# Per-example mixing matrices: one batch on TensorE at the front, or two VectorE operations inside each step

## The chip, the cores and the metric

The kernel runs on one core of a Trainium2 chip. The metric is device time in microseconds (us). Before the change it is 2982.37 us, the median of 3 runs (2981.94 to 2983.42). Engines are named as in the profile: PE is TensorE (PEld its weight loads), DVE is VectorE, ACT is ScalarE, POOL is GpSimd, SP is SyncE, which only issues DMAs (SPq).

## What is computed

There are 128 examples x[j] of 128 channels by 2048 time points, in float32. Each passes four residual layers. Layers 0 and 2 mix the channels with a matrix of the example's own: eight fixed 128x128 matrices, weighted by a softmax of a small MLP on the example's condition. Layers 1 and 3 are grouped convolutions of 9 taps over time.

```
h   = gelu(gelu(cond @ W0 + b0) @ W1 + b1)
att = softmax(h @ W2 + b2)                           # 8 weights an example
agg_w = einsum('bk,koi->boi', att, weight[..., 0])   # the example's matrix
agg_b = att @ bias_k
x = x + einsum('boi,bih->boh', agg_w, x) + agg_b     # layers 0 and 2
x = x + conv(x, weight, 9 taps, 4 groups) + cond @ c_weight.T + side   # layers 1 and 3
```

## The kernel before, in words

**Tiling.** Every tensor is split into a high part (rounded to the type that TensorE multiplies at speed) and a low part (the rest), and each product is three passes: high by high, high by low, low by high. Four 32-row tiles of the array work side by side (t = 0 to 3), each three rounds behind the one before. One layer's result for one example is four banks of 128x512: mixing layers use banks 0 to 3, convolutions banks 4 to 7. A step has 96 rounds of 4 matmuls: 12 for layer 0, 36 for layer 3, 12 for layer 2, 36 for layer 1. The identity of each residual is inside the weights.

**Steps.** Step i works on layers 0 and 1 of example i, layer 2 of example i-1 and layer 3 of example i-2. Steps -1 to 2 and 126 to 129 are unrolled, and a hardware loop runs the rest. Each engine has its own program in a fixed order, and semaphores tie them. In step i:

- DVE writes the low parts of layer 1 (`low(1, i-1)`) and of layer 0 (`low(0, i)`), four operations each (L587); then `x_high(i+1)`, four casts of the next example (L596), which wait for its load; then `low(2, i-1)`.
- ACT evacuates the high parts (L438), casts both mixing matrices (L444) and evacuates layer 3 into `o_ph` (L464), which raises `phases_set`.
- POOL writes the matrices' low parts (L628), `x_low(i+1)` (four operations, L635), and `in_time(i-2)` (L642), which puts the result into time order in `o_t`.
- SP issues, in this order: four loads of layer 2's matrix (L198), the 16 shuffles of example i-2 that bring `o_ph` to `o_ch` (L228, after `phases_set`), `load_x(i+2)` (four DMAs, L203, after `x_low(i+1)` has freed `x_t`), four loads of layer 0's matrix, the store of the output (L236).

**Mixing matrices.** All 256 of them are made before the first step. The attention is transposed and masked; TensorE multiplies 64 times (L279) with eight kernels' matrices laid over the partitions; ACT (L412) and DVE (L558) evacuate the results into stages of 2 MB; DVE adds the diagonal (L564); SP stores eight such stages into the scratch `mixed` in DRAM (L194). The steps then load 64 KB four times a matrix. The stages, the small inputs and the output buffers share the tile `work`.

Of the kernel before, what the change touches and what calls it, by code (L numbers as in the profile page):

```python
# [5 lines left out]
def build_cond_resid(nc, x, small, mix_w, mix_b, conv_w, consts, scratch, out):  # L6
# [7 lines left out]
    PH = 4  # L14
# [5 lines left out]
    SMALL = small.shape[1]  # L20
    NL = 4
    Q = 4
    QW = C * C // Q
    QB = QW // N
# [3 lines left out]
    LOADS = 3  # L28
    CHUNKS = 4

    ctx = ExitStack()
    with ctx:
# [12 lines left out]
        work = sb("work", [128, 5, QW])  # L45
        o_ph = work[:, 0, 0:T].rearrange("c (g n) -> c g n", g=G)
        o_ch = work[:, 0, T:2 * T].rearrange("c (p n) -> c p n", p=PH)
        o_t = work[:, 1, 0:T]
        m_raw = {l: sb(f"m_raw{l}", [128, G, C]) for l in (0, 2)}
        m_parts = {l: sb(f"m_parts{l}", [128, 2, G, C], f32r) for l in (0, 2)}  # L50
        bias = [sb(f"bias{l}", [128, G]) for l in range(NL)]
        conv_parts = {l: sb(f"conv_parts{l}", [128, 2, SHIFTS, 128], f32r) for l in (1, 3)}
        bias_table = sb("bias_table", [128, B, NL * G])
        ps = ctx.enter_context(nc.psum_tensor("ps", [128, 8, N], fp32))


        conv_raw = sb("conv_raw", [128, SHIFTS * 128])
        consts_sb = sb("consts_sb", [128, 166])
        ident = consts_sb[:, 0:128]
        w_low = consts_sb[:, 128:129]  # L60
        a_low = consts_sb[:, 129:130]
        in_quarter = consts_sb[:, 130:134]
        ident_g = consts_sb[:, 134:166]

# [4 lines left out]
        mix_raw = [work[:, 2, :], work[:, 4, :]]  # L69
        mix_high = flat(xp, "r g n")  # L70
        mix_parts = flat(y1, "r p n")[:, 0:QW]
        room_r = flat(y2, "r g n")
        room = work[:, 3, :]

        stage = [work[:, k, :] for k in range(5)]
        SLOT = (0, 1, 3, 2, 3, 4, 2, 4)
        taken = {"room": 0, "room_r": 0}
        def part_of(name, shape):

            width = 1  # L80
            for n in shape[1:]:
                width *= n
            first = taken[name]
            taken[name] += width
            view = (room if name == "room" else room_r)[0:shape[0], first:first + width]
# [5 lines left out]
        emb_sb = part_of("room", [128, B])  # L91
        mlp_w_sb = part_of("room", [128, 4, 128])
        ctx_w_sb = part_of("room", [128, 2, G, 128])
        mlp_b_sb = part_of("room", [128, 4])
        w2_sb = part_of("room", [128, 2, K])
        b2_sb = part_of("room", [128, 2, K])
        side_sb = part_of("room", [128, G])
        assert taken["room"] == SMALL
        mix_b_sb = part_of("room", [K, 2, 128])
        hidden0 = part_of("room", [128, 2, B])  # L100
        hidden1 = part_of("room", [128, 2, B])
        att_rep = part_of("room", [128, 2, 128])
        att_t = part_of("room", [128, 2, B])
        att_high = part_of("room_r", [128, 2, B])
        att_parts = part_of("room_r", [128, 2, B])
        att_q = part_of("room_r", [128, 2, Q, B])
# [5 lines left out]
        small_in = sem("small_in")  # L112
        mix_in = [sem(f"mix_in{l}") for l in range(2)]
        conv_in = sem("conv_in")

        hid0_mm, ctx_mm, hid1_mm = sem("hid0_mm"), sem("ctx_mm"), sem("hid1_mm")
        logit_mm, att_t_mm, mix_b_mm = sem("logit_mm"), sem("att_t_mm"), sem("mix_b_mm")
        agg_mm = sem("agg_mm")

        hid0_set, hid1_set, expo_set = sem("hid0_set"), sem("hid1_set"), sem("expo_set")  # L120
        mix_high_set, conv_high_set = sem("mix_high_set"), sem("conv_high_set")
        agg_act = sem("agg_act")
# [3 lines left out]
        att_t_set, att_q_set, mix_b_read = sem("att_t_set"), sem("att_q_set"), sem("mix_b_read")  # L126
        mix_set, conv_ident_set, conv_set = sem("mix_set"), sem("conv_ident_set"), sem("conv_set")
        agg_dve = sem("agg_dve")
        agg_set = sem("agg_set")
        zeros_set = sem("zeros_set")  # L130
        stored = [sem(f"stored{s}") for s in range(len(stage))]
# [13 lines left out]
        in_time_set = sem("in_time_set")  # L145

# [22 lines left out]
        def uses(n):  # L169

            return SLOT[:n].count(SLOT[n])

        def by_phase(q):

            return ps[:, q, :].rearrange("c (m p) -> c p m", p=PH)

# [7 lines left out]
        def _(sp):  # L184
            sp.dma_start(room[:, 0:SMALL], small).then_inc(small_in, 16)
            sp.dma_start(consts_sb[:], consts).then_inc(small_in, 16)
            sp.dma_start(mix_b_sb, mix_b).then_inc(small_in, 16)
            sp.dma_start(mix_raw[0], mix_w[0]).then_inc(mix_in[0], 16)
            sp.dma_start(conv_raw[:], conv_w[0]).then_inc(conv_in, 16)
            sp.dma_start(mix_raw[1], mix_w[1]).then_inc(mix_in[1], 16)  # L190

            def store_quarter(n):
                sp.wait_ge(agg_set, n + 1)
                sp.dma_start(scratch[n // Q][:, n % Q * QW:(n % Q + 1) * QW], stage[SLOT[n]]).then_inc(stored[SLOT[n]], 16)  # L194

            def load_matrix(layer, j):
                for q in range(G):
                    sp.dma_start(m_raw[layer][CG * q:CG * (q + 1)],  # L198
                                 scratch[layer // 2][bass.ds(j, 1)].rearrange("s (g c o) -> (s c) g o", g=G, c=CG)).then_inc(m_in[layer], 16)

# [4 lines left out]

            load_x(0)
            for n in range(Q):
                store_quarter(n)
            sp.wait_ge(conv_set, 1)
            sp.dma_start(conv_raw[:], conv_w[1]).then_inc(conv_in, 16)  # L210
            for n in range(Q):
                sp.wait_ge(stored[SLOT[n]], 16 * (uses(n) + 1))
            for n in range(Q, 2 * Q):
                store_quarter(n)
            for n in range(Q, 2 * Q):
                sp.wait_ge(stored[SLOT[n]], 16 * (uses(n) + 1))
            load_matrix(0, 0)
# [27 lines left out]
        def _(pe):  # L245
# [27 lines left out]
            for n in range(2 * Q):  # L273
                for m in range(QB):
                    if m % (QB // CHUNKS) == 0:
                        pe.wait_ge(mix_set, n // Q * CHUNKS + m // (QB // CHUNKS) + 1)
                    if n:
                        mixed_out(n - 1, m)
# [471 lines left out]
```

## Time and profile before

| | |
|---|---|
| median of 3 runs | 2982.37 us |
| the profiled execution, own time | 2982.91 us |
| its span | 2981.1 us |
| busy share of the span: PE, DVE, ACT, POOL | 97%, 44%, 52%, 52% |
| mean granted TensorE clock | 0.985 of full speed |
| DMA | 493.88 MB, 166 GB/s |

A busy share says how long an engine was at work, not whether something waited for it. The page's line of 40 slices has PE at 9 tenths from the second slice on; only the first slice (4) and the last (7) are lower. An operation's mean duration times its count is its busy time, and the idle time before a group, with its releaser, says what it waited for.

### The profile page before, as it was taken

To read this page: it belongs to the slowest core of one execution; us is meant where nothing else is said; L and a number is where in the kernel's file an instruction comes from. 1 tells how busy PE (TensorE), PEld (TensorE's weight loads), DVE (VectorE), ACT (ScalarE), POOL (GpSimd) and SP (SyncE) were. 2 spreads that over 40 slices of the span, in tenths; PEclk is the share of its full clock that TensorE was granted. 3 is DMA by queue.
4 is the path that set the end of the run, shared out by engine and by line. 5 is a ranking of instruction groups with operands and counts; after the bars stand their busy time and mean duration, and the time that the engine had idled before them with its cause. 6 is when DMAs were issued, how large, how long until landed. Compare 5 with 4: busy or idle time off the path is not lost.

```text
span 2981.1 us, 121239 instructions
## 1 busy us (share of the span) xinstructions
PE 2905.9 (97%) x49252; PEld 2885.6 (97%) x49252; DVE 1312.3 (44%) x2142; ACT 1552.4 (52%) x2358; POOL 1551.1 (52%) x1796
## 2 busy tenths in 40 slices
PE   4899999999999999999999999999999999999997
PEld 2799999999999999999999999999999999999996
DVE  5344444444444444444444444444444444444441
ACT  4455555555555555555555555555555555555552
POOL 0455555555555555555555555555555555555552
PEclk7899999999999999999999999999999999999998
DMA  7465665665665665665665655655655656656653
GB/s 312 106 178 157 163 173 157 165 171 158 165 170 158 166 169 158 167 168 158 171 164 158 173 162 158 175 160 158 178 157 159 179 156 161 178 155 162 176 156 110
DMA packets 339978, 493.88 MB, mean 166 GB/s; under 512 B 59624, under 2 KB 190832, under 8 KB 322288
## 3 DMA queue, kind: packets, MB, share of 16 engines
q1 hardware_dynamic: 339952, 493.51, 60.9%
q8 instruction: 19, 0.31, 0.0%
q14 instruction: 7, 0.06, 0.0%
HBM read 208.06 MB, written 150.99 MB: 120 GB/s over the span
## 4 chain that ended last, share of the span: by engine, by line
PE 97%; DMA 1%; DVE 1%; ACT 0%; SPq 0%; issue 0%; POOL 0%; POOLq 0%; DVEq 0%; ACTq 0%
PE ps L317 72%; PE ps L302 24%; DMA mixed<-work 1%; DMA conv_raw<-conv_w 0%; SPq L228 0%; DVE work L558 0%; ACT work L412 0%; DVE y L542 0%; DVE y L587 0%; PE ps L279 0%; DMA work<-mix_b 0%; ACT xp L399 0%; PE ps L251 0%; POOL work L642 0%; DMA m_raw<-mixed 0%
## 5 line engine op out<-in xcount | busy, mean ns | idle before, releaser
L317 PE MATMUL ps<-y,conv_parts 32*128 32x512 f32 x36864 | 2667.9, 390 | 3.2 <-DVE y L587 3.2
L317 PEld LDWEIGHTS ps<-y,conv_parts 32*128 32x128 f32 x36864 | 2547.7, 184 | 9.1 <-DVE y L587 4.1
L587 DVE SCALAR_TENSOR_TENSOR y<-ps,bias,y 128x512 fp32r<-128x512 f32 x1536 | 1085.3, 750 | 1446.9 <-ACT y L438 1440.2
L438 ACT ACTIVATE y<-ps,bias 128x512 fp32r<-128x512 f32 x1536 | 1046.4, 690 | 683.8 <-PE ps L317 646.3
L635 POOL TENSOR_TENSOR xp<-x_t,xp 128x512 fp32r<-128x512 f32 x512 | 647.0, 1300 | 0.0
L302 PE MATMUL ps<-xp,m_parts 32*128 32x512 f32 x6144 | 621.1, 391 | 24.2 <-POOL xp L635 24.2
L628 POOL TENSOR_TENSOR m_parts<-m_raw,m_parts 128x512 fp32r<-128x512 f32 x256 | 331.7, 1296 | 585.5 <-ACT m_parts L444 585.4
L302 PE MATMUL ps<-y,m_parts 32*128 32x512 f32 x6144 | 618.9, 390 | 0.1
L302 PEld LDWEIGHTS ps<-xp,m_parts 32*128 32x128 f32 x6144 | 560.7, 184 | 25.9 <-issue 24.4
L302 PEld LDWEIGHTS ps<-y,m_parts 32*128 32x128 f32 x6144 | 562.2, 183 | 0.7 <-issue 0.5
L624 POOL COPY bias<-bias_table 128x4 f32 (+1 forms) x512 | 102.0, 200 | 816.5 <-DMA work<-work 662.5
L642 POOL COPY work<-work 128x512 f32<-128x512 f32 x512 | 513.1, 1124 | 23.5 <-DMA work<-work 23.5
L464 ACT ACTIVATE work<-ps,bias 128x512 f32<-128x512 f32 x512 | 330.3, 687 | 320.4 <-PE ps L317 317.3
L444 ACT CAST m_parts<-m_raw 128x512 fp32r<-128x512 f32 x256 | 157.6, 616 | 368.0 <-DMA m_raw<-mixed 368.0
L596 DVE CAST xp<-x_t 128x512 fp32r<-128x512 f32 x512 | 184.7, 424 | 160.1 <-DMA x_t<-x 160.1
L279 PE MATMUL ps<-y 128*128 128x512 f32 x64 | 24.8, 532 | 19.7 <-ACT work L412 14.4
L279 PEld LDWEIGHTS ps<-y 128*128 128x128 f32 x64 | 14.1, 249 | 30.4 <-issue 18.1
L412 ACT COPY work<-ps 128x512 f32<-128x512 f32 x32 | 17.0, 603 | 15.2 <-DMA mixed<-work 9.4
L558 DVE COPY work<-ps 128x512 f32<-128x512 f32 x32 | 20.0, 683 | 8.0 <-DMA mixed<-work 7.8
L404 ACT CAST conv_parts<-conv_raw 128x1536 fp32r<-128x1536 f32 x2 | 2.9, 1472 | 14.3 <-DVE conv_raw L499 14.3
L542 DVE SCALAR_TENSOR_TENSOR y<-xp,consts_sb,work 128x1024 fp32r<-128x1024 f32 x8 | 9.7, 1280 | 0.0
L399 ACT CAST xp<-work 128x4096 fp32r<-128x4096 f32 x2 | 7.2, 3614 | 0.0
(38 smaller groups left out, 37.3 us busy)
## 6 DMA issues: line engine op xcount, KB each, us to landing
x_t<-x SPq DMA_DIRECT2D x512, 256.0 KB, 5.1
work<-work SPq DMA_DIRECT2D x2048, 64.0 KB, 2.0
out<-work SPq DMA_DIRECT2D x128, 1024.0 KB, 4.8
m_raw<-mixed SPq DMA_DIRECT2D x1024, 64.0 KB, 4.4
mixed<-work SPq DMA_DIRECT2D x8, 2048.0 KB, 7.9
work<-mix_w SPq DMA_DIRECT2D x2, 2048.0 KB, 12.7
conv_raw<-conv_w SPq DMA_DIRECT2D x2, 768.0 KB, 10.8
work<-small SPq DMA_DIRECT2D x1, 852.0 KB
```

The source lines that it names most:

```text
L279: nc.tensor.matmul(ps[:, m, :], att_q[:, n // Q, n % Q, :], mix_parts[:, m * N:(m + 1) * N], start=True, stop=True).then_inc(agg_mm, 1)
L302: ins = nc.tensor.matmul(ps[:, t, :], m_parts[layer][rows, m, g, :], src[rows, a, g, :], start=(k == 0), stop=(k == MIX - 1))
L317: ins = nc.tensor.matmul(ps[:, 4 + t, :], conv_parts[layer][rows, w, s, :], src[rows, a, p_in, q:q + N], start=(k == 0), stop=(k == CONV - 1))
L438: nc.scalar.activation(dst, src, ACT.Identity, bias=bias[layer][:, k:k + 1]).then_inc(high_set[layer], 1)
L444: nc.scalar.copy(m_parts[layer][:, HIGH], m_raw[layer][:]).then_inc(m_high_set[layer], 1)
L464: nc.scalar.activation(o_ph[:, g, :], ps[:, 4 + g, :], ACT.Identity, bias=bias[3][:, g:g + 1]).then_inc(phases_set, 1)
L587: nc.vector.scalar_tensor_tensor(out=dst, in0=src, scalar=bias[layer][:, k:k + 1], in1=high.bitcast(fp32), op0=ALU.add, op1=ALU.subtract). ...
L596: nc.vector.tensor_copy(xp[:, HIGH, g, :], x_t[:, g, :]).then_inc(x_high_set, 1)
L624: nc.gpsimd.tensor_copy(bias[layer][:], bias_table[:, bass.ds(j, 1), layer * G:(layer + 1) * G].rearrange("c j g -> c (j g)")).then_inc(bi ...
L628: nc.gpsimd.tensor_tensor(m_parts[layer][:, LOW], m_raw[layer][:], m_parts[layer][:, HIGH].bitcast(fp32), ALU.subtract).then_inc(m_set[lay ...
L635: nc.gpsimd.tensor_tensor(xp[:, LOW, g, :], x_t[:, g, :], xp[:, HIGH, g, :].bitcast(fp32), ALU.subtract).then_inc(x_low_set, 1)
L642: nc.gpsimd.tensor_copy(ov[:, p, :], o_ch[:, p, :]).then_inc(in_time_set, 1)
```

## The change

**Matrices.** The 64 matmuls, their evacuations, masks, diagonal and 2 MB stores go. A table `att_table` holds for each example and mixing layer its eight weights on every partition and a ninth entry of 1. It comes from 16 matmuls of a broadcast weight column with the identity, evacuated by ACT and DVE. `mix_sb` holds for each of 128 input channels the 128x9 values (eight matrices and the identity). In step i DVE makes `matrix(0, i+2)` and `matrix(2, i+1)`, each a product of 128x1152 (L524) and a sum over the innermost nine (L530), between `x_high(i+1)` and `low(2, i-1)`. SP stores each result (64 KB) to the scratch, and the loads of `m_raw` stay.

**SP's order.** In step i: loads of layer 0's matrix i+1, loads of layer 2's matrix i, the output of example i-3, the store of layer 0's matrix i+2 (after DVE's sum), the shuffles of example i-2, the store of layer 2's matrix i+1, `load_x(i+2)`.

**Front.** Smaller first loads, x before the weights; x's casts first on DVE; a Gelu on a spare element at the start; the context matmuls later; the second convolution's weights are prepared inside step 0, by POOL and ACT.

**Convolutions.** The 12 shifts are taken input phase by input phase, three at a time, and layer 3 waits for each phase of `y3` when it comes to it, where it waited for all four. Layer 1 still waits for all.

**Last example.** ACT and DVE write the four phases of each of its output groups straight into time order in `x_t` (two phases each, 32 rows by 512), and four DMAs of 256 KB store it. No shuffles, no `in_time`.

**Biases.** Mixing layers have one bias column, not four.

```diff
+            def store_matrix(layer, j):
+                sp.wait_ge(summed[layer], j + 1)
+                sp.dma_start(scratch[layer // 2][bass.ds(j, 1)].rearrange("s c o -> (s c) o"), m_sum[layer][:]).then_inc(stored[layer], 16)
...
             def step(i, inner):
+                if has(i, inner, -1):
+                    load_matrix(0, i + 1, not inner and i == -1)
                 if has(i, inner, 0):
-                    if inner or i >= 1:
-                        sp.wait_ge(m_set[2], i)
-                    load_matrix(2, i)
-                if has(i, inner, 2):
+                    load_matrix(2, i, not inner and i == 0)
+                if has(i, inner, 3):
+                    sp.wait_ge(in_time_set, 4 * (i - 2))
+                    sp.dma_start(out[i - 3], o_t[:]).then_inc(out_done, 16)
+                if has(i, inner, -2):
+                    store_matrix(0, i + 2)
+                if has(i, inner, 2) and (inner or not is_last(i)):
                     for g in range(G):
                         sp.wait_ge(phases_set, nth(i - 2, g))
                         for p in range(PH):
                             sp.dma_start(o_ch[CG * g:CG * (g + 1), p, :], o_ph[CG * p:CG * (p + 1), g, :]).then_inc(shuffled[p], 16)
+                if has(i, inner, -1):
+                    store_matrix(2, i + 1)
                 if has(i, inner, -2):
                     sp.wait_ge(x_low_set, 4 * (i + 2))
                     load_x(i + 2)
-                    sp.wait_ge(m_set[0], i + 2)
-                    load_matrix(0, i + 2)
-                if has(i, inner, 2):
-                    sp.wait_ge(in_time_set, 4 * (i - 1))
-                    sp.dma_start(out[i - 2], o_t).then_inc(out_done, 16)
...
+            def matrix(layer, j, first):
...
+                nc.vector.tensor_tensor(prod[layer][:], mix_sb[layer][:],
+                                        att_table[:, bass.ds(j, 1), l, :].broadcast_to([128, C, K + 1]),
+                                        ALU.mult).then_inc(scaled[layer], 1)
+                dve.wait_ge(scaled[layer], j + 1)
...
+                nc.vector.tensor_reduce(m_sum[layer][:], prod[layer][:], AX_X, ALU.add).then_inc(summed[layer], 1)
...
-                if has(i, inner, -1):
-                    x_high(i + 1, not inner and i == -1)
+                if now and has(i, inner, -1):
+                    x_high(i + 1, False)
+                if has(i, inner, -2):
+                    matrix(0, i + 2, False)
+                if has(i, inner, -1):
+                    matrix(2, i + 1, not inner and i == -1)
```

SP's program in the hardware loop, before: from the last group of shuffles (`work<-work`) to the store of the output. `phases_set` comes from ACT, `x_low_set` and `m_set0` from POOL.

```order
L228 DMA work<-work 32x512 [waits phases_set]
L228 DMA work<-work 32x512 x3
L230 ISA
L203 ISA [waits x_low_set]
L203 DMA x_t<-x 32x4x512
L203 ISA
L203 DMA x_t<-x 32x4x512
L203 ISA
L203 DMA x_t<-x 32x4x512
L203 ISA
L203 DMA x_t<-x 32x4x512
L198 ISA [waits m_set0]
```

The same queue in the changed kernel, from the output's store to the first group of shuffles (now `o_ch<-o_ph`); `summed0` comes from DVE's sum.

```order
L216 ISA [waits in_time_set]
L216 DMA out<-o_t 128x2048
L183 REGISTER_ALU
L184 ISA [waits summed0]
L184 DMA mixed<-m_sum 128x128
L221 REGISTER_ALU
L223 DMA o_ch<-o_ph 32x512 [waits phases_set]
L223 DMA o_ch<-o_ph 32x512 x3
```

The shuffles now stand behind a store that waits for DVE. Behind the last group of shuffles the changed queue goes on with the second store and the load of x:

```order
L223 DMA o_ch<-o_ph 32x512 [waits phases_set]
L223 DMA o_ch<-o_ph 32x512 x3
L184 ISA [waits summed2]
L184 DMA mixed<-m_sum 128x128
L227 REGISTER_ALU
L178 ISA [waits x_low_set]
L178 DMA x_t<-x 32x4x512
```

One more DMA stands between the shuffles and the load of x. On DVE, the loop before has this between the low parts of layer 0 and those of layer 2 (`high_set2`, from ACT):

```order
L592 ISA
L594 ISA [waits x_in]
L596 CAST xp<-x_t 128x512 [waits mm0]
L596 CAST xp<-x_t 128x512 x3
L587 SCALAR_TENSOR_TENSOR y<-ps,bias,y 128x512 [waits high_set2] x4
```

And after the change, from the same wait for x:

```order
L488 ISA [waits x_in]
L490 CAST xp<-x_t 128x512 [waits mm0]
L490 CAST xp<-x_t 128x512 x3
L524 ISA [waits summed0]
L524 TENSOR_TENSOR prod<-mix_sb,att_table 128x1152
L527 REGISTER_ALU
L529 REGISTER_ALU [waits scaled0]
L530 TENSOR_REDUCE m_sum<-prod 128x128 [waits stored0]
L524 ISA [waits summed2]
L524 TENSOR_TENSOR prod<-mix_sb,att_table 128x1152
L529 REGISTER_ALU [waits scaled2]
L530 TENSOR_REDUCE m_sum<-prod 128x128 [waits stored2]
```

Four operations stand behind the casts of x and ahead of `low(2, i-1)`.

## Rows read from the trace of the kernel before

**Rows 1.** The page: the chain that ended last, by engine.
```profile
PE 97%; DMA 1%; DVE 1%; ACT 0%; SPq 0%; issue 0%; POOL 0%; POOLq 0%; DVEq 0%; ACTq 0%
```
**Rows 2.** One step by engine: busy us (count), PEclk, DMA share, GB/s.
```profile
1300.00:1322.30 22.30, 22.30 (x389) 22.30 (x386) 9.91 (x16) 11.87 (x18) 12.08 (x15) 1.00 0.62 165
```
**Rows 3.** Timeline of DVE: start, length, instructions, and the idle time before them.
```profile
1305.08 5.68 DVE L587 SCALAR_TENSOR_TENSOR y<-ps,bias,y 128x512 fp32r<-128x512 f32 x8 [5.47 <-ACT y L438]
1311.92 1.43 DVE L596 CAST xp<-x_t 128x512 fp32r<-128x512 f32 x4 [1.16 <-DMA x_t<-x]
1319.05 2.85 DVE L587 SCALAR_TENSOR_TENSOR y<-ps,bias,y 128x512 fp32r<-128x512 f32 x4 [5.69 <-ACT y L438]
1327.38 5.68 DVE L587 SCALAR_TENSOR_TENSOR y<-ps,bias,y 128x512 fp32r<-128x512 f32 x8 [5.47 <-ACT y L438]
1334.39 1.43 DVE L596 CAST xp<-x_t 128x512 fp32r<-128x512 f32 x4 [1.33 <-DMA x_t<-x]
```
**Rows 4.** Timeline of PE: the first matmul of layer 0 in that step.
```profile
1304.16 0.40 PE L302 MATMUL ps<-xp,m_parts 32*128 32x512 f32 x1
```
**Rows 5.** Timeline of SP's queue in the same step.
```profile
1304.47 1.85 SPq L203 DMA_DIRECT2D x_t<-x  x4
...
1316.46 10.04 SPq L228 DMA_DIRECT2D work<-work  x16
1326.77 1.85 SPq L203 DMA_DIRECT2D x_t<-x  x4
```
**Rows 6.** Timeline of POOL: layer 0's matrix and x's low parts.
```profile
1313.44 1.30 POOL L628 TENSOR_TENSOR m_parts<-m_raw,m_parts 128x512 fp32r<-128x512 f32 x1 [2.31 <-ACT m_parts L444]
1314.68 5.06 POOL L635 TENSOR_TENSOR xp<-x_t,xp 128x512 fp32r<-128x512 f32 x4
...
1335.76 1.30 POOL L628 TENSOR_TENSOR m_parts<-m_raw,m_parts 128x512 fp32r<-128x512 f32 x1 [2.33 <-ACT m_parts L444]
```
**Rows 7.** Groups by form, 0 to 140 us: busy us, mean ns, idle before.
```profile
L549 DVE TENSOR_TENSOR conv_parts<-conv_raw,conv_parts 128x1536 fp32r<-128x1536 f32 x2 | 3.5, 1754 | 1.5 <-ACT conv_parts L404 1.5
L510 DVE TENSOR_REDUCE top<-logits 128x1 f32<-128x8 f32 x2 | 0.3, 161 | 0.1
```
**Rows 8.** Timeline of DVE in an early step.
```profile
128.78 2.52 DVE L596 CAST xp<-x_t 128x512 fp32r<-128x512 f32 x4
```
**Rows 9.** Timeline of POOL beside it.
```profile
129.65 1.37 POOL L628 TENSOR_TENSOR m_parts<-m_raw,m_parts 128x512 fp32r<-128x512 f32 x1 [0.41 <-ACT m_parts L444]
```
**Rows 10.** The chain that ended last, front: start, length, what.
```profile
12.15 0.40 ACT expo L387 x2
...
78.88 0.34 SPq L198
...
82.43 0.63 ACT m_parts L444
83.12 1.26 POOL m_parts L628
```
**Rows 11.** Timeline of PE: the first matmuls of the first step.
```profile
85.75 7.59 PE L302 MATMUL ps<-xp,m_parts 32*128 32x512 f32 x48 [24.15 <-POOL xp L635]
```
**Rows 12.** The front in stretches, columns as in rows 2.
```profile
0.00:6.00 6.00, 0.39 (x2) 0.40 (x3) 0.00 (x0) 0.00 (x0) 0.20 (x4) 1.00 0.69 229
6.00:12.00 6.00, 5.04 (x28) 4.76 (x27) 3.09 (x14) 3.68 (x6) 0.00 (x0) 1.00 0.94 371
12.00:24.00 12.00, 7.15 (x18) 4.21 (x19) 10.35 (x27) 8.31 (x18) 4.45 (x4) 0.57 0.88 283
```
**Rows 13.** Timeline of PE: layer 3 of the last example.
```profile
2948.80 13.07 PE L317 MATMUL ps<-y,conv_parts 32*128 32x512 f32 x144 [1.66 <-DVE y L587]
```
**Rows 14.** Timeline of ACT: the last evacuation.
```profile
2960.36 2.42 ACT L464 ACTIVATE work<-ps,bias 128x512 f32<-128x512 f32 x4 [12.49 <-PE ps L317]
```
**Rows 15.** Timeline of SP's queue: the last shuffles and the last store.
```profile
2961.08 10.35 SPq L228 DMA_DIRECT2D work<-work  x16
2976.93 0.34 SPq L236 DMA_DIRECT2D out<-work  x1
```

More of the change, by code:

```diff
@@ L73, in build_cond_resid, with part_of @@
[L73 to L78, printed above, removed]
+        room = sb("room", [128, small.shape[1]])
+        taken = [0]
+        def part_of(shape):
             width = 1
@@ L217, in _, with load_matrix @@
-            load_matrix(0, 0)
+            def store_matrix(layer, j):
+                sp.wait_ge(summed[layer], j + 1)
+                sp.dma_start(scratch[layer // 2][bass.ds(j, 1)].rearrange("s c o -> (s c) o"), m_sum[layer][:]).then_inc(stored[layer], 16)
+            def load_matrix(layer, j, first):
+                if not first and layer == 0:
+                    sp.wait_ge(m_set[layer], j)
+                sp.wait_ge(stored[layer], 16 * (j + 1))
+                if not first and layer == 2:
+                    sp.wait_ge(m_set[layer], j)
+                for q in range(G):
+                    sp.dma_start(m_raw[layer][CG * q:CG * (q + 1)],
+                                 scratch[layer // 2][bass.ds(j, 1)].rearrange("s (g c) o -> (s c) g o", g=G)).then_inc(m_in[layer], 16)
@@ L456, in step @@
                 if before:
+                    final = not inner and is_last(i)
                     for g in range(G):
@@ L596, in x_high, with conv_identity @@
                     nc.vector.tensor_copy(xp[:, HIGH, g, :], x_t[:, g, :]).then_inc(x_high_set, 1)
+            def conv_identity(layer):
+                dve.wait_ge(conv_in[layer], 16)
+                shifts = conv_raw[layer][:].rearrange("p (s m) -> p s m", s=SHIFTS)
+                for p in range(PH):
+                    own = shifts[:, PH + p, CG * p:CG * (p + 1)]
+                    last = nc.vector.tensor_tensor(own, own, ident_g, ALU.add)
+                last.then_inc(conv_ident_set, 1)
@@ new lines, in _, with low @@
+            conv_identity(1)
+            att_rows(0)
+            matrix(0, 0, True)
+            for l in range(2):
+                dve.wait_ge(att_t_mm, l + 1)
+                nc.vector.tensor_copy(att_t[:, l, :], ps[0:K, l, 0:B]).then_inc(att_t_set, 1)
+            att_rows(1)
+            conv_low_part(1)
+            def low(layer, j, k, dst, src, high):
+                dve.wait_ge(high_set[layer], nth(j, k))
+                nc.vector.scalar_tensor_tensor(out=dst, in0=src, scalar=bias[layer][:, k % WIDTH[layer]:k % WIDTH[layer] + 1],
+                                               in1=high.bitcast(fp32), op0=ALU.add, op1=ALU.subtract).then_inc(low_set[layer], 1)
@@ L653, in step @@
                     matrix_low(0, i + 1)
+                if not inner and i == 0:
+                    conv_low_part(3)
+                if now and has(i, inner, -1):
                     x_low(i + 1)
@@ L659, in step @@
                     matrix_low(2, i)
-                if before:
+                if before and (inner or not is_last(i)):
                     if inner or i > 2:
@@ L667, in step @@
                     set_bias(2, i)
-                if before:
+                if before and (inner or not is_last(i)):
                     in_time(i - 2)
+            pool.wait_ge(first_in, 32)
+            x_low(0)
+            pool.wait_ge(mix_b_read, 2)
+            pool.wait_ge(ctx_read, 2)
             for layer in range(NL):
                 set_bias(layer, 0)
+            conv_identity(3)
             steps(step)
```

455 lines of the change are left out of this document (204 added, 251 removed).

## The prediction

> **What bounds the kernel now.** I read the chain that ended last first: 97% of it is PE [rows 1]. One step by engine then shows PE busy for all of its 22.30 us at full granted clock, while DVE has 9.91 us, ACT 11.87 and POOL 12.08 [rows 2]; DVE starts the same operation again after 22.30 us [rows 3]. So a step costs 22.30 us as long as everything else gets round in that time, and nothing that the change does makes PE's 384 matmuls of a step fewer. What it can win lies at the two ends; what it can lose lies in a step that no longer gets round.
>
> **Front: about 61 us less.** Before, the first matmul of the first step starts at 85.75 [rows 11], because the matrices of all examples are made and stored first: layer 0's first matrix is asked for at 78.88 and cast at 82.43 [rows 10]. Afterwards only one matrix is needed. The inputs are some 4.7 MB; at the rates of the first 12 us (6 us at 229 GB/s, 6 us at 371: 3.6 MB) and 283 GB/s behind [rows 12] all are in by 16 us, and the 2.9 MB up to layer 0's weights by about 10. The softmax's exponential stood at 12.15 [rows 10]; the context matmuls leave its way, x's casts enter it, so I keep about 12. Then come 8 matmuls and two evacuations (some 2 us), and the product and sum (2.7 us, below): the sum is there at about 17. Its store takes an estimated 2.5 us, the load as before 3.55 (78.88 to 82.43), the cast and the low part 1.95 (82.43 to 83.12 plus 1.26) [rows 10]: the first matmul at about 25, 60 to 61 us sooner, and with x's low parts ready the first 48 matmuls are not paced by POOL as in their 7.59 us [rows 11], worth up to 2 us. I take 61, bounds 56 to 64.
>
> **Tail: about 13 us less.** After the last evacuation starts (2960.36) [rows 14] come 16 shuffles, POOL's reordering, and a store issued at 2976.93 [rows 15] that ends with the span at 2981.1. Afterwards ACT writes eight pieces at its pitch of 0.6 us (2.42 for four), DVE as many beside it: 4.8 us. The final store's 256 KB takes somewhat less than the 4.2 us that 1 MB took; I take 3.8 with the issue. That ends at 2969. The wait before the last convolution (1.66 us) [rows 13] mostly goes, since it now needs one phase and not four: 2967.7. I take 13, bounds 10 to 15.
>
> Without any effect on the steps this gives 2982.9 (the profiled execution's own time, 0.5 above the median of the runs) - 61 - 13 = 2909.
>
> **Steps: a loop that is longer than PE's 22.30 us.** Per step DVE gets two products and two sums. The trace has no such operation of 1152 elements; two VectorE rows give a straight line, 161 ns for 8 elements and 1754 for 1536 [rows 7]: 1.04 ns each and 0.153 us fixed, so 1.35 us for 1152, 2.74 us for a product, a hand-over of 0.04 and a sum, 5.5 us for both matrices. Counted as busy time that is free: DVE goes to 15.4 of 22.30. In its program it also seems to fit, since between the casts' end at 1313.35 and `low(2)` at 1319.05 there are 5.7 us of waiting for ACT [rows 3]. The cost is in the order of SP's queue. SP may not start the shuffles before it has stored layer 0's new matrix; DVE may not make that before it has cast x; and x is loaded behind the shuffles of the step before. That is a circle with one turn a step:
>
> - from the first issue of x's load to the first cast: 7.45 us (1304.47 to 1311.92) and 7.62 (1326.77 to 1334.39) [rows 3, 5]: 7.53
> - casts until the product can start: 1.34 (1.43 less the overlap of neighbours)
> - product, hand-over, sum: 2.74
> - SP wakes, computes an address, issues the store: 0.49
> - 16 shuffles: 10.04 [rows 5]
> - the second store's issue 0.45, and 0.27 until x's first load (1326.50 to 1326.77) [rows 5]
>
> Together 22.86. To this I add 0.1 for the second store's 64 KB ahead of x in the DMA queue (between nothing and 0.5, a sixteenth of the 7.53 us that x's megabyte takes; most of those are latency), and a share of the following.
>
> At 128.78 the four casts took 2.52 us and not 1.43; POOL's subtraction of 1.37 us ran from 129.65 to 131.02 [rows 8, 9], and the casts ended 0.28 after it. So the two engines can exclude each other for the length of an operation, here for 1.09 us. The Trainium skill (SBUF — State Buffer, Who interferes with whom) says that a VectorE instruction with two SBUF inputs contends with a GpSimd instruction that reads SBUF, and that the second to issue blocks until the first is done; by that rule the new products, whose inputs both lie in SBUF, are exposed, and the sums are not. No row here shows a product beside POOL, only casts.
>
> POOL's subtraction for layer 0's matrix starts 1.52 us and 1.37 us after the first cast [rows 3, 6], the product would start at 1.34. DVE is ahead by 0.03 to 0.18 us. If it is always first, the circle gets nothing; if it is always second, 1.09 to 1.30 us. I take once in seven, 0.15. The circle is then 23.1 us, bounds 22.7 and 24.2, and it exceeds PE's step by 0.8 us.
>
> The excess first eats slack. If x is cast at its present place, `low(2)` would have its first bank free at 1311.92 + 1.34 + two matrices 5.5 + 0.75 = 1319.5, and PE needs that bank at 1304.16 + 22.30 = 1326.46 [rows 3, 4]: 6.9 us. POOL's last x_low has a little more. The first turns with shuffles start 0.55 us late. So over the 124 turns from step 3 on: 124 x 0.8 + 0.55 - 6.9 = 93 us. 2909 + 93 = 3002.
>
> **What costs nothing.** The extra stores are 128 KB on 3.9 MB a step; the DMA share of a step is 0.62 [rows 2]. The later loads of layer 2's matrix stand before the output's store in a stretch where SP waits. The new order of shifts has the same matmuls. Narrower biases are not on any wait. If PE is idle for under a microsecond a step I expect its granted clock to stay at 1.00.
>
> **Rivals.** A: the circle gets round in 22.30 us. For it: its excess without POOL is only 0.56 us on a sum of eight terms, and DVE's gap seems to fit. It needs x's load in 7.0 us, which neither step shows. Time: 2909, faster by 2.5%. B: the circle is only slightly long, 22.4 to 22.8, because x lands sooner or SP's addresses are computed while it waits: 124 x 0.3 - 6.4 = 31 on 2909, so 2940. C, on the far side: POOL is first at the shared interface in most turns, because the matrix lands as early beside x as now and DVE's product comes a moment later; from 1 turn in 2 on, the circle is 23.5 and more (124 x 1.2 - 6.4 = 142, 3051), and in every turn 24.1 (217 us, 3126). D: PE's order of shifts slows its matmuls; nothing in the rows speaks for it, since the rate is the same in both layers, and I give it nothing.
>
> **Numbers.** Chances: the circle at 22.8 to 23.4 us, 0.48; A 0.24; B 0.13; C 0.15. The time is that of the first, 3002; its own range is 2965 to 3045. The range for all reaches from A to C's middle, 2905 to 3070. What a measurement here can tell from no change is 0.2%, 2976.4 to 2988.3. Faster is A, B and the lower edge of the first (a circle under 22.9): 0.40. Within 0.2% is a circle of 22.9 to 23.0: 0.10. Slower: 0.50.
>
> **What would show it.** In a step late in the loop: DVE starts its casts every 23.1 us and not every 22.30; SP's store of layer 0's matrix starts right after DVE's sum and the first shuffle right after it, with `phases_set` long there; PE has an idle time of about 0.8 us a step before layer 0, released by DVE. The first matmul of layer 0 stands at 25 us, and the span ends 7 to 9 us after the last evacuation's start. A trace with PE busy throughout at a period of 22.30 makes the circle wrong and A right; products of 2.5 us and more make C right. I would be wrong altogether if the shuffles' issue is faster than 10.04 us once their buffers are tiles of their own.

## The result, and the profile after the change

The changed kernel takes 3061.91 us (median of 4 runs, 3059.13 to 3062.92), against 2982.15 us before: a ratio of 1.0265, 95% interval 1.0247 to 1.0283. It is slower by 80 us. The profiled execution took 3059.13 us with a span of 3057.3 us.

The page's chain by engine, which answers to [rows 1], has turned over. PE was 97% of it:

```profile
SPq 47%; DMA 25%; DVE 16%; issue 7%; PE 3%; DVEq 1%; POOL 0%; ACT 0%; ACTq 0%
```

SP's queue, the DMA of x and DVE now carry the run. The busy time of one stretch by engine, columns as in [rows 2] (PE, PEld, DVE, ACT, POOL, granted clock, DMA share, GB/s):

```profile
1323.60:1347.20 23.60, 22.82 (x393) 22.31 (x389) 15.93 (x21) 11.21 (x18) 13.94 (x14) 1.00 0.62 165
```

The clock stays at full speed. PE is idle 0.78 us of 23.60. DVE is at 15.93, far from full, so its busy time alone explains nothing. Its timeline, which answers to [rows 3] (start, length, instruction, idle before):

```profile
1300.48 1.43 DVE L490 CAST xp<-x_t 128x512 fp32r<-128x512 f32 x4 [6.12 <-DMA x_t<-x]
1301.83 1.35 DVE L524 TENSOR_TENSOR prod<-mix_sb,att_table 128x1152 f32<-128x1152 f32 x1
1303.31 1.35 DVE L530 TENSOR_REDUCE m_sum<-prod 128x128 f32<-128x1152 f32 x1
1304.58 2.23 DVE L524 TENSOR_TENSOR prod<-mix_sb,att_table 128x1152 f32<-128x1152 f32 x1
1306.93 1.35 DVE L530 TENSOR_REDUCE m_sum<-prod 128x128 f32<-128x1152 f32 x1
...
1323.87 1.43 DVE L490 CAST xp<-x_t 128x512 fp32r<-128x512 f32 x4 [5.98 <-DMA x_t<-x]
```

The casts come 23.39 us apart, where they came every 22.3 us. DVE waits 6 us for x in each turn, five times as long as before, though its own work in a turn has grown from 9.9 us to 15.9. SP's queue over the same stretch, which answers to [rows 5]:

```profile
1304.83 0.37 SPq L184 DMA_DIRECT2D mixed<-m_sum  x1
1305.31 10.05 SPq L223 DMA_DIRECT2D o_ch<-o_ph  x16
1315.55 0.44 SPq L184 DMA_DIRECT2D mixed<-m_sum  x1
1316.25 1.89 SPq L178 DMA_DIRECT2D x_t<-x  x4
```

These two views close the circle, that is, the chain that leads from an instruction back to the same instruction one turn later: the first sum ends at 1304.66, the store that waited for it is issued at 1304.83, the shuffles behind it at 1305.31, x's load at 1316.25, and the casts start again 7.62 us later at 1323.87. Of SP's waits, longest in total, two say the same (us in total, times, longest):

```profile
SPq L184 <- DVE m_sum L530: 636.0, 131, 16.9
...
SPq L223 <- ACT o_ph L459: 10.7, 5, 3.9
```

Before, the shuffles' wait for ACT was SP's longest:

```profile
SPq L228 <- ACT work L464: 327.1, 128, 8.2
```

Now it is the sum that holds SP, and `phases_set` has long been there.

The whole difference by parts, from the two traces: the first matmul of layer 0 starts at 32.13 and not at 85.75 [rows 11], 53.6 us less. From the last evacuation's start to the end of the span it is 3057.3 - 3044.43 = 12.9 us and not 20.7 [rows 14], 7.9 less. The part between them took 2874.6 us and takes 3012.3, 137.7 more. Together +76.2, which is the difference of the two profiled executions, 3059.13 and 2982.91. PE's recorded waits for ACT make up 102.1 us of the 137.7, 0.84 a step where the step is 1.1 longer; the rest lies inside PE's recorded busy time, whose ends the profile models.

### The profile page after: what moved, and what is told of

It is laid out like the page before. It is cut to its first block, busy times and chain, and to the rows that moved or that the text cites. A ratio compares the mean times of both kernels' runs of the same rounds, so it can differ in the third digit from the quotient of the medians.

```text
span 3057.3 us, 123405 instructions
## 1 busy us (share of the span) xinstructions
PE 2919.7 (95%) x49220; PEld 2803.7 (92%) x49220; DVE 2050.8 (67%) x2587; ACT 1458.8 (48%) x2333; POOL 1789.0 (59%) x1801
## 4 chain that ended last, share of the span: by engine, by line
SPq 47%; DMA 25%; DVE 16%; issue 7%; PE 3%; DVEq 1%; POOL 0%; ACT 0%; ACTq 0%
SPq L223 37%; DMA x_t<-x 24%; DVE m_sum L530 6%; SPq L178 5%; DVE prod L524 5%; DVE xp L490 5%; SPq L184 4%; PE ps L306 2%; PE ps L291 1%; SPq L221 1%; DMA m_raw<-mixed 0%; ACT x_t L456 0%; POOL xp L626 0%; DVEq L488 0%; DVEq L529 0%
## 5 line engine op out<-in xcount | busy, mean ns | idle before, releaser
L306 PE MATMUL ps<-y,conv_parts 32*128 32x512 f32 x36864 | 2743.1, 390 | 104.2 <-ACT o_ph L459 102.1
L306 PEld LDWEIGHTS ps<-y,conv_parts 32*128 32x128 f32 x36864 | 2495.4, 184 | 206.1 <-issue 154.1
L626 POOL TENSOR_TENSOR xp<-x_t,xp 128x512 fp32r<-128x512 f32 x512 | 788.7, 1573 | 9.3 <-DVE xp L490 9.3
L619 POOL TENSOR_TENSOR m_parts<-m_raw,m_parts 128x512 fp32r<-128x512 f32 x256 | 447.5, 1748 | 534.2 <-ACT m_parts L430 534.2
L291 PE MATMUL ps<-y,m_parts 32*128 32x512 f32 x6144 | 684.7, 396 | 0.0
L633 POOL COPY o_t<-o_ch 128x512 f32<-128x512 f32 x508 | 502.8, 1110 | 10.3 <-DMA o_ch<-o_ph 10.3
L615 POOL COPY bias<-bias_table 128x4 f32 (+3 forms) x512 | 90.3, 194 | 705.3 <-DMA o_ch<-o_ph 662.8
L524 DVE TENSOR_TENSOR prod<-mix_sb,att_table 128x1152 f32<-128x1152 f32 x256 | 459.2, 1794 | 0.1
L530 DVE TENSOR_REDUCE m_sum<-prod 128x128 f32<-128x1152 f32 x256 | 346.3, 1353 | 31.0
L459 ACT ACTIVATE o_ph<-ps,bias 128x512 f32<-128x512 f32 x508 | 308.3, 686 | 15.7 <-PE ps L306 15.4
```

Source lines behind the costliest of these rows:

```text
L291: ins = nc.tensor.matmul(ps[:, t, :], m_parts[layer][rows, m, g, :], src[rows, a, g, :], start=(k == 0), stop=(k == MIX - 1))
L306: ins = nc.tensor.matmul(ps[:, 4 + t, :], conv_parts[layer][rows, w, PH * q + p_in, :], src[rows, a, p_in, q:q + N], start=(k == 0), stop= ...
L459: nc.scalar.activation(o_ph[:, g, :], ps[:, 4 + g, :], ACT.Identity, bias=bias[3][:, g:g + 1]).then_inc(phases_set, 1)
L524: nc.vector.tensor_tensor(prod[layer][:], mix_sb[layer][:], att_table[:, bass.ds(j, 1), l, :].broadcast_to([128, C, K + 1]), ALU.mult).the ...
L530: nc.vector.tensor_reduce(m_sum[layer][:], prod[layer][:], AX_X, ALU.add).then_inc(summed[layer], 1)
L619: nc.gpsimd.tensor_tensor(m_parts[layer][:, LOW], m_raw[layer][:], m_parts[layer][:, HIGH].bitcast(fp32), ALU.subtract).then_inc(m_set[lay ...
```

## The experiments

All ratios are against the kernel before on the same chip, with 95% intervals. Four runs each.

### Opening the circle at two places

**e1: SP stores layer 0's matrix behind the shuffles.**

```diff
-                if has(i, inner, -2):
-                    store_matrix(0, i + 2)
                 if has(i, inner, 2) and (inner or not is_last(i)):
                     ...
+                if has(i, inner, -2):
+                    store_matrix(0, i + 2)
                 if has(i, inner, -1):
                     store_matrix(2, i + 1)
```

> The changed kernel with one edit: SP issues the store of layer 0's new matrix behind the 16 shuffles, just ahead of layer 2's, and not ahead of them. Nothing else. Theory (the circle of x's load, casts, product, sum, store, shuffles, load sets the step): the shuffles no longer wait for DVE, the circle is open, DVE's casts come every 22.30 us again and PE has no idle time in a step. The middle part of the run loses the 138 us that it gained, so about 2921 us. Rival (DVE's products and POOL's subtractions exclude each other, and POOL's late low parts or the two engines' added work set the step): the same products stand beside the same POOL work, so no change within 10 us of 3061.

Measured: 2922.94 us, ratio 0.9798 (0.9782 to 0.9815). The move of one DMA is worth 139 us. DVE, POOL and SP do the same work as in the changed kernel:

```profile
1309.46 1.43 DVE L490 CAST xp<-x_t 128x512 fp32r<-128x512 f32 x4 [2.50 <-DMA x_t<-x]
1310.81 1.35 DVE L524 TENSOR_TENSOR prod<-mix_sb,att_table 128x1152 f32<-128x1152 f32 x1
...
1313.56 2.23 DVE L524 TENSOR_TENSOR prod<-mix_sb,att_table 128x1152 f32<-128x1152 f32 x1
```

The second product still takes 2.23 us beside POOL, so the exclusion of the two engines is as it was, and it costs nothing. The part between the first matmul (33.78) and the last evacuation (2908.06) takes 2874.3 us, as it did before (2874.6). So the extra work on DVE, the extra stores, the new order of the shifts and the narrower biases together cost nothing that shows once the circle is open. PE is busy again for the whole of a step:

```profile
1300.00:1322.30 22.30, 22.30 (x392) 21.45 (x388) 15.85 (x20) 11.90 (x18) 14.10 (x14) 1.00 0.65 170
```

**e2: DVE makes the matrices ahead of x's casts.**

```diff
-                if now and has(i, inner, -1):
-                    x_high(i + 1, False)
                 if has(i, inner, -2):
                     matrix(0, i + 2, False)
                 if has(i, inner, -1):
                     matrix(2, i + 1, not inner and i == -1)
+                if now and has(i, inner, -1):
+                    x_high(i + 1, False)
```

> The changed kernel with one edit: DVE makes both matrices ahead of x's casts, and not behind them. SP's order stays. Theory: the sum no longer waits for x, so the store ahead of the shuffles is there before phases_set (sum of layer 0 about 9.5 us into PE's step, the shuffles at 12.3), the circle is open at another place, and the step is 22.30 us: about 2921 us. x is cast some 4 us later in the step, which its slack covers. Rival (the order of SP's queue by itself is too long, whatever DVE does; or DVE's added work is what costs): stays at about 3061.

Measured: 2922.50 us, ratio 0.9795 (0.9779 to 0.9811). SP's order is untouched, and the time is that of e1. So neither the queue's order nor DVE's order is slow by itself: only both together close the circle. Here the sum is stored at 1309.24 and the shuffles wait for ACT until 1311.99.

### Is it in the circle, or only on the same engine?

**e3 and e4: half of layer 0's product and sum, or half of layer 2's.**

```diff
+                H = C // 2 if layer == 0 else C        # e4: layer == 2
-                nc.vector.tensor_tensor(prod[layer][:], mix_sb[layer][:],
+                nc.vector.tensor_tensor(prod[layer][:, 0:H], mix_sb[layer][:, 0:H],
...
-                nc.vector.tensor_reduce(m_sum[layer][:], prod[layer][:], AX_X, ALU.add)
+                nc.vector.tensor_reduce(m_sum[layer][:, 0:H], prod[layer][:, 0:H], AX_X, ALU.add)
```

> The changed kernel, but DVE makes layer 0's matrix for 64 of the 128 input channels only (product and sum over 576 elements and not 1152; the other half of the matrix is zero). It leaves out half of that matrix. Theory: 2 x 576 elements x 1.04 ns = 1.20 us go from the circle, 23.45 becomes 22.25, just under PE's 22.30: about 2925 us, and certainly under 2940. Rival (port exclusion): the product's exclusion of POOL gets 0.6 us shorter, worth at most 0.6 us a step, 75 us: 2985.

> The changed kernel, but DVE makes layer 2's matrix for 64 of the 128 input channels only, with the same saving of 1.20 us of DVE's work a step. It leaves out half of that matrix. Theory: that work is behind layer 0's sum on DVE and not in the circle, so no change: 3061 within 5 us. Rivals (DVE's total work a step, or low(2) being late, or port exclusion): as much as in the case of layer 0, 75 to 130 us faster.

Measured: 2920.55 us for layer 0, ratio 0.9791 (0.9774 to 0.9807); 3064.12 us for layer 2, ratio 1.0271 (1.0254 to 1.0288). The same 1.2 us of DVE's work is worth 141 us in one place and nothing in the other, two operations further down the same engine. DVE's total work a step is out as the cause, since both edits lower it alike. (Each leaves out half of one matrix.) The exclusion of DVE and POOL they do not lower alike: layer 2's product is held up 0.22 us in e3 (1.57 us long for 1152 elements) and 0.88 in e4 (1.63 for 576). That it is not the cause is shown by e1, which has all of it and no idle PE.

**e9: layer 0's sum twice.**

```diff
+                if layer == 0 and not first:
+                    nc.vector.tensor_reduce(spare_sum[:], prod[layer][:], AX_X, ALU.add)
                 nc.vector.tensor_reduce(m_sum[layer][:], prod[layer][:], AX_X, ALU.add).then_inc(summed[layer], 1)
```

> The changed kernel, but DVE does layer 0's sum twice in each step (the first copy goes to a spare tile). Theory: one more sum of 1.35 us less the overlap of neighbours (1.27 us at the pitch seen) in the circle, each turn that much longer, 124 turns: 3061 + 157 = about 3218 us. Rival (DVE has 6 us of waiting for x a turn that the sum can use, as total work suggests): 3061.

Measured: 3223.16 us, ratio 1.0807 (1.0789 to 1.0825), 161 us more than the changed kernel (157 expected). DVE has 7.48 us of waiting for x in the turn shown and could not use it, because the wait is itself part of the circle:

```profile
1299.92 1.43 DVE L491 CAST xp<-x_t 128x512 fp32r<-128x512 f32 x4 [7.48 <-DMA x_t<-x]
...
1324.57 1.43 DVE L491 CAST xp<-x_t 128x512 fp32r<-128x512 f32 x4 [5.83 <-DMA x_t<-x]
```

**e10: x's load ahead of the second store.**

```diff
+                if has(i, inner, -2):
+                    sp.wait_ge(x_low_set, 4 * (i + 2))
+                    load_x(i + 2)
                 if has(i, inner, -1):
                     store_matrix(2, i + 1)
-                if has(i, inner, -2):
-                    sp.wait_ge(x_low_set, 4 * (i + 2))
-                    load_x(i + 2)
```

> The changed kernel with one edit: SP issues the load of x directly behind the shuffles and the store of layer 2's matrix behind it, and not the other way round. Theory: the second store's issue and its gap leave the circle, 0.89 us from the last shuffle's end to x's first DMA become 0.27, so 0.62 us x 124 = 77 us less: about 2984 us; up to 15 us less still if the store's 64 KB also kept x waiting in the DMA queue. Rival (it is only SP's total number of DMAs): 3061.

Measured: 2962.90 us, ratio 0.9933 (0.9916 to 0.9949): 99 us less than the changed kernel, 22 more than the issue alone explains. From the casts' start at 1309.99 to the next at 1332.58 it is 22.59 us. SP's rows show the gap of 0.27 us that I had counted on:

```profile
1314.82 10.03 SPq L223 DMA_DIRECT2D o_ch<-o_ph  x16
1325.12 1.90 SPq L178 DMA_DIRECT2D x_t<-x  x4
1327.20 0.38 SPq L184 DMA_DIRECT2D mixed<-m_sum  x1
```

The two traces say where the rest is. Over 104 turns of the loop, the time from x's first load to the first cast is 7.67 us on average in the changed kernel and 7.52 in e10: 0.15 us a turn, 18 us over the run, and the 15 us that I had allowed for the store's 64 KB in x's way was a little small. That it is the bytes of that store, and not something else about its place, was not tried apart.

### Which wait brings the circle to PE

**e11: ACT evacuates layer 3 ahead of layer 0's matrix cast.**

```diff
-                if has(i, inner, -1):
-                    matrix_high(0, i + 1, not inner and i == -1)
                 if before:
                     final = not inner and is_last(i)
                     ...
+                if has(i, inner, -1):
+                    matrix_high(0, i + 1, not inner and i == -1)
```

> The changed kernel with one edit: ACT evacuates layer 3 into o_ph ahead of layer 0's matrix cast (which waits for a load behind x's), and not behind it. Theory: this wait decided only after how many turns the circle reached PE, not its length. The turn stays 23.4 us; the slack grows from about 4 us to nearly 7, once: 2 to 3 us less, about 3058, and PE's idle time moves from layer 1's convolution to layer 0's mixing. Rival (ACT's order is what makes each step longer, since PE's idle time of 0.8 us a step ends with ACT's evacuation): 0.8 to 1.1 us a step go, about 2930.

Measured: 3058.82 us, ratio 1.0256 (1.0239 to 1.0273). That is 3 us under the changed kernel, of the size expected, but the two intervals overlap, so the time alone does not show it. The waits do. PE's idle time in the changed kernel and in e11:

```profile
PE ps L306 <- ACT o_ph L459: 102.1, 122, 1.4
```

```profile
PE ps L291 <- DVE y L554: 105.7, 121, 1.9
```

About the same idle time, 0.84 and 0.87 us a step, stands at another instruction, with another releaser, and the step is as long. The engine named as PE's releaser was never the cause.

### The front

**e5: attention and first matrix ahead of x's casts (on e1). e6: on POOL, also the first matrix's low part ahead of biases and identity additions.**

```diff
             dve.wait_ge(first_in, 32)
-            x_high(0, True)
             ...
             matrix(0, 0, True)
+            x_high(0, True)                 # e5; in e6 behind att_t's two copies
...
             x_low(0)
+            matrix_low(0, 0)                # e6
             pool.wait_ge(mix_b_read, 2)
```

> Kernel e1 (store behind the shuffles), and at the front DVE casts the first example only after the attention and layer 0's first matrix, and not before them. Theory: the softmax no longer waits for x and for four casts that POOL's subtractions hold up (3.56 us where 1.43 is their length); the first sum comes about 7 us earlier, but POOL still has four bias copies and four identity additions ahead of the first low part, so the first matmul comes some 5 to 6 us earlier: about 2917 us against e1's 2923. Rival (the first loads bound the front: layer 0's weights land at about 14 us and everything follows them): under 2 us.

> Kernel e1 with the whole front reordered: attention and first matrix ahead of x's casts, and on POOL the first matrix's low part ahead of the first biases and of the second convolution's identity additions. Theory: the two delays add up, first matmul at about 25 us where e1 has it at 33.8: about 2914 us. Rival (POOL's order costs nothing because ACT's bias tables are late anyway): as in the case with the attention alone, 2917.

Measured: 2920.34 us, ratio 0.9792 (0.9776 to 0.9809), and 2919.47 us, ratio 0.9785 (0.9769 to 0.9801). That is 2.6 and 3.5 us under e1, half of what I expected or less. The intervals overlap, so the time alone does not show a gain. The first matmul starts at 30.88 and 29.81 where e1 has 33.78, and the runs that leave the front as it is have it between 32.05 (e9) and 34.51 (e10), with x landing sooner or later. The sum did come 7.5 us sooner (16.57 against 24.02 in e1), but POOL was late. The four subtractions of x's low parts, POOL in e5 and in the changed kernel:

```profile
18.41 8.38 POOL L626 TENSOR_TENSOR xp<-x_t,xp 128x512 fp32r<-128x512 f32 x4 [17.04 <-DVE xp L490]
```

```profile
10.71 5.32 POOL L626 TENSOR_TENSOR xp<-x_t,xp 128x512 fp32r<-128x512 f32 x4 [9.33 <-DVE xp L490]
```

They now ran beside DVE's products, and 3 us were lost to the exclusion.

**e12: e6 with x's casts between attention and first matrix, and at the tail the last example's first store ahead of the output of the example before it.**

```diff
+            x_high(0, True)
             conv_identity(1)
             att_rows(0)
             matrix(0, 0, True)
...
                         sp.dma_start(out[i - 2][CG * g:CG * (g + 1)], ...)
+                        if g == 0:
+                            sp.wait_ge(in_time_set, 4 * (i - 2))
+                            sp.dma_start(out[i - 3], o_t[:]).then_inc(out_done, 16)
```

> Kernel e1 with a new front and tail: on DVE the attention first, then x's casts, then the first matrix; on POOL the first matrix's low part ahead of biases and identity additions; the last example's first store ahead of the store of the example before it. Theory: POOL's low parts of x are done before DVE's products begin, so neither holds the other up; first matmul at 25 to 26 us where e1 has 33 to 34 and e6 29.8: 4 us less than e6, up to 1 us less at the tail, about 2915. Rival (the first matmul is followed by waits for the next matrices, which still come one behind the other): 2919 as e6.

Measured: 2919.87 us, ratio 0.9791 (0.9774 to 0.9807), the same as e6. The expectation failed: the first matmul starts at 30.75. POOL's subtractions were free of the products, but DVE's casts and small additions were held up beside them, so the sum came at 21.00:

```profile
10.76 3.57 DVE L493 CAST xp<-x_t 128x512 fp32r<-128x512 f32 x4 [1.33 <-DMA x_t<-x]
14.25 2.62 DVE L501 TENSOR_TENSOR conv_raw<-conv_raw,consts_sb 128x32 f32<-128x32 f32 x4
```

The four additions of 32 elements are 0.49 us long in the changed kernel. The three orders of the front end within 1 us of each other. e1, e2, e5, e6 and e12 all beat both kernels; of these e6 has the lowest median, with no clear lead over the others.

### The tail

**e7: the last pieces written without the step of four elements (on e1). e8: the last example on the old way (on e1).**

```diff
-            return ....rearrange("c (n p) -> c p n", p=PH)[:, p, :]
+            return ....rearrange("c (p n) -> c p n", p=PH)[:, p, :]       # e7
...
-            return i - 2 == B - 1
+            return False                                                  # e8, and one more store of out[B - 1]
```

> Kernel e1, but the last example's pieces are written one behind the other and not interleaved with a step of four elements; its output is in phase order (that is left wrong). Theory: the step of four elements makes each 32x512 piece cost 1.15 us where a contiguous 128x512 costs 0.69; contiguous pieces take 0.65 to 0.7, the eight of each engine 5 us and not 9.4, and the run is about 4 us shorter, 2919. Rival (the price is that of a 32-row piece, or of two engines writing one tile): pieces stay at 1.1 us and the time at 2923.

> Kernel e1, but the last example goes the way of all others (o_ph, 16 shuffles, POOL's reordering, one store), which undoes the change's second part. Theory: from the start of the last evacuation to the end of the span 20.7 us as in the kernel before, where e1 has 12.4: 8 us more, about 2931. Rival (the straight way gains nothing, since its pieces take 9.4 us and its stores come late): 2923 within 3.

Measured: e7 2921.60 us, ratio 0.9794 (0.9777 to 0.9810); e8 2934.66 us, ratio 0.9837 (0.9821 to 0.9854). The straight way is worth 11.7 us (8 expected). In e8 it takes 24.7 us from the start of the last evacuation (2908.93) to the end, not the 20.7 of the kernel before, because SP's new order puts the output of the example before ahead of the last shuffles:

```profile
2912.74 0.34 SPq L216 DMA_DIRECT2D out<-o_t  x1
2913.12 10.82 SPq L221 DMA_DIRECT2D o_ch<-o_ph  x16
```

The shuffles start 4.2 us after that evacuation, where they started 0.7 us after it [rows 14, 15].

e7 leaves the last output in phase order. Its expectation is right on the pieces and wrong on the time. ACT's eight pieces in e1 and in e7:

```profile
2908.06 9.39 ACT L456 ACTIVATE x_t<-ps,bias 32x512 f32<-32x512 f32 x8 [7.46 <-PE ps L306]
```

```profile
2908.19 5.60 ACT L456 ACTIVATE x_t<-ps,bias 32x512 f32<-32x512 f32 x8 [7.46 <-PE ps L306]
```

But 12.4 us from there to the end became 12.6. In e7 the pieces are done at 2914.5 (DVE's), but SP is at the issue of the last of its four stores until 2917.2:

```profile
2912.09 0.34 SPq L216 DMA_DIRECT2D out<-o_t  x1
...
2913.95 1.55 SPq L233 DMA_DIRECT2D out<-x_t  x1
...
2915.60 1.57 SPq L233 DMA_DIRECT2D out<-x_t  x1
```

These two issues take 1.55 and 1.57 us and not 0.34. They follow each other closely behind the 1 MB output of the example before; in e12 three such stores behind the same output, some 2.3 us apart at the pieces' pace, took at most 0.35 us each. What holds an issue up is not shown. So at the tail two limits seem to lie side by side, the pieces' pace and the issue of the stores, and taking away one leaves the other. At the tail e12 changed the order of the stores alone and kept the slow pieces: 2905.08 to 2917.5, again 12.4. The two together were not tried.

## Why the prediction came out as it did

Right, with the trace's word on each:

- The mechanism: a circle through SP's queue, x's load and DVE, longer than PE's step. e1, e2, e3, e4 and e9 each move the time by what the circle gives, within some 5 us, and e10 within 22, where DVE's or SP's total would give something else.
- The rival A, that 22.86 us of rough terms might be 22.30, is out: the circle takes 23.43, and even e10's, shorter by one store's issue, is at 22.66 over the loop. The rival C, POOL ahead of DVE, is out too, though the mechanism exists. The product right behind x's casts is 1.35 or 1.36 us long in all of the 127 turns that have one, because DVE is first, and POOL's subtraction waits:

```profile
1302.17 2.18 POOL L619 TENSOR_TENSOR m_parts<-m_raw,m_parts 128x512 fp32r<-128x512 f32 x1 [4.37 <-ACT m_parts L430]
1304.30 6.18 POOL L626 TENSOR_TENSOR xp<-x_t,xp 128x512 fp32r<-128x512 f32 x4
```

  Before they took 1.30 and 5.06 [rows 6], and the second product is 2.23 us long where it is second. By the rule of the Trainium skill (SBUF — State Buffer, Who interferes with whom) the two exclude each other and the one that issues first wins; the trace agrees, 0.88 us each way, and the sums beside POOL are 1.35 us throughout, as the rule has it.
- The lengths of the products and sums: 1.35 us forecast from two rows of other sizes, 1.35 measured.

Wrong, and this is why 3002 was 60 us too low, and the loss 80 us where 20 were forecast:

- **The circle's length. This is the step that failed: its hand-overs were sized too small.** Forecast 23.1, of which 0.15 was for POOL and 0.1 for the second store's data. Measured from 174.93 to 2588.05 it is 23.43 over 103 turns. The traces give it in three parts, as averages over the loop. From the first cast to the first shuffle it is 4.83 us and not 4.57: in the turn shown 0.13 between product and sum (1303.18 to 1303.31) instead of the 0.04 that I had put without a row for it, and 0.65 from the sum's end to the first shuffle instead of 0.49 (1304.66 to 1305.31). From the first shuffle to x's load it is 10.93 and not 10.76, because a gap of 0.19 between the last shuffle and the second store was left out (1315.36 to 1315.55). From x's load to the cast it is 7.67 and not 7.53, which the 0.1 for the second store's data nearly covers. The share for POOL should have been nothing. So hand-overs and gaps that were 0.43 us too small, against 0.15 for POOL that never came, make nearly all of the 0.33 us that each turn is longer. Over 124 turns that is 41 us, of the 57 that the forecast was too low for the profiled execution.
- **The slack.** I had 6.9 us before PE would feel the circle, from `low(2)`. With turns of 23.43 the part between the ends should then have grown by 134 us, and it grew by 138, some 4 us more. Part of that may be the first turns, which are longer than the rest (24.70 from 103.04 to 127.74); part is less slack, and e11 shows one reason for it. In the changed kernel layer 3's evacuation stands behind the cast of layer 0's matrix, whose load comes behind x's, and layer 1's convolution waits for the bank; PE's first such wait falls between 130 and 160 us, and with ACT's order changed the first wait of the loop, now for DVE, falls between 160 and 190. But the part between the ends is only 1.2 us shorter in e11 (33.43 to 3044.52), so how the 4 us divide stays open. I had named what is queued behind DVE's new work and not what is queued behind the late load on ACT.
- **The front, 53.6 us and not 61.** I had kept the exponential at 12.15; it is at 14.31, because the casts in front of the logits take 3.56 us beside POOL's subtractions and not 1.43, the same exclusion that I had used only for the steps. The larger part is the way from the exponential to the first product, 6.67 us (14.31 to 20.98): I had given matmuls and evacuations some 2 us, and they run from 16.11 to 20.85. The table evacuation takes 1.12 us and not 0.7. From the sum's end to the first matmul it is 8.4 us where I had 8, though POOL spends 2.0 us on the second convolution's identity just before the first low part.
- **The tail, 7.9 us and not 13.** I took the pace of contiguous 128x512 evacuations, 0.6 us, for pieces that are written with a step of four elements; they take 1.15, which e7 shows to be the step's price. With contiguous pieces alone the gain would have been no larger, by e7.

Together: 41 from the circle, 4 from slack and first turns, 7 and 5 from the ends make up the 57 us (3059 measured, 3002 forecast, for the profiled execution). The range, 2905 to 3070, held the time only because rival C, which was not the cause, had stretched it. That is luck: the forecast's own range ended at 3045.

## What to carry to other kernels

When work is put into a loop, busy time does not tell whether it fits. Look for every circle that the new waits close across engines and queues, from an instruction back to the same instruction one turn later, and compare its length with the step; an in-order DMA queue with a waiting instruction in front of others is the usual place where it closes. A hundredth of a microsecond forgotten in such a circle is paid in every turn, so take each hand-over from a row of its own, and open the circle before shortening it: moving one DMA issue was worth 139 us. An engine that shows idle time in front of the circle's longest wait has no room, and the releaser that the profile names at the engine that starves may be only the place where the circle arrives.

## What the runs showed of the hardware that I had not expected

- A write to SBUF with a step of four fp32 elements costs 1.6 times a contiguous one on ACT: 1.15 us a piece of 32x512 against 0.70 (9.39 and 5.60 us for eight), and 1.5 times on DVE, 1.15 against 0.78 (9.17 and 6.24). The table evacuations of 128x512, also with a wide step, take 1.12. The Trainium skill (SBUF — State Buffer, Door 1: The DMA port swizzle) has lines of 16 bytes and a penalty for each access that crosses to a new one; a step of four fp32 elements touches a new line with each element, and e7 agrees with it. No run tried a shorter step, so the line itself is not shown.
- DVE's cast of four times 128x512 took 1.43 us alone and 3.56 beside POOL's subtractions at the front, and four additions of 32 elements 2.62 us beside them and not 0.49. For small operations such a meeting can cost a multiple of their length. It does not always: in e6 the four casts took 1.41 us although POOL's subtractions began 0.56 us behind them, about as in e5, where they took 3.55. Why the two differ is open. e6's rows:

```profile
18.53 1.41 DVE L490 CAST xp<-x_t 128x512 fp32r<-128x512 f32 x4
19.09 8.29 POOL L626 TENSOR_TENSOR xp<-x_t,xp 128x512 fp32r<-128x512 f32 x4 [17.72 <-DVE xp L490]
```

- The issue of a DMA from SP is not free: 0.63 us for each of the 16 shuffles of 64 KB in the loop (10.05 for all), 0.65 at the tail of the kernel before (10.35). Most single issues shown take 0.34 to 0.44 us, and two in e7, close behind a store of 1 MB, took 1.55 and 1.57; what held them is not shown.
